# FFN weights loaded and first channels mixed sooner, a new place for the last two weights, and the last pair's gate columns ahead of the former pair's experts

## What is computed

```python
# 1 a long convolution per token channel h (64 of them) over the 1024 features, masked by a length
y = irfft(rfft(u_m, n) * rfft(kernel(h), n))[..., :L] + u_m * D[:, None];  y = y * mask
# 2 grouped-query attention, 32 query heads, 8 key/value heads of 32, causal, sequences of 64
q, k, v = y @ Wq.T, y @ Wk.T, y @ Wv.T;  q, k = rope(q), rope(k)
x = x + softmax(q @ k.T / sqrt(32) + causal) @ v @ Wo.T
# 3 channel mixing: each sequence's 64 tokens mixed by one of 16 matrices of 64 x 64
xf = einsum('bct,bcd->bdt', x, weights[condition])
# 4 a linear layer with a mixture of 8 rank-8 experts, the 2 best by a softmax gate
w = top2(softmax(xf @ gate_W.T)) normalised
x = x + xf @ W_base.T + einsum('ter,eor->to', (xf @ A) * w * 2.0, B)
```

## Time and profile before

| What | Value |
|---|---|
| Median of three runs (lowest to highest) | 924.44 us (922.88 to 925.8) |
| The profiled execution: its own time | 924.91 us |
| Its span in the profile | 922.8 us |
| TensorE busy | 881.5 us, 96% |
| VectorE, GpSimd, ScalarE busy | 446.4, 395.5, 202.4 us |
| Output store of 512 KB, issue to landing | 2.6 us, median |
| Store to the x1 scratch of 512 KB, issue to landing | 3.1 us, median |
| Instruction queues (q8 and q14) | 107 packets, 1.6 MB, 0.3% of the DMA time |

### The profile page before, as it was taken

The page is one execution under the profiler, slowest core; times in us unless marked ns, Lnnn a source line. Parts: engine busy times, 40 slices in busy tenths (PEclk is TensorE's granted clock), DMA queues, the critical chain, the costliest instruction groups (busy, mean ns, idle before and its releaser), DMA issues.

```text
span 922.8 us, 24871 instructions
## 1 busy us (share of the span) xinstructions
PE 881.5 (96%) x11040; PEld 766.8 (83%) x11040; DVE 446.4 (48%) x935; ACT 202.4 (22%) x363; POOL 395.5 (43%) x294
## 2 busy tenths in 40 slices
PE   0899999999999999999999999999999999999997
PEld 0789899988888888888777777777779999999997
DVE  7455663111222222259887776788514444334444
ACT  4334552200000000023123222233322111011010
POOL 1234555301555656569978877867511000000000
PEclk9999999999999999999999989999999999999999
DMA  2678878412223323256544544643343221212201
GB/s 65 150 190 205 203 177 191 119 46 69 69 77 97 78 69 75 51 172 178 152 138 138 154 140 137 180 133 113 136 132 107 70 92 47 92 70 70 93 24 69
DMA packets 81931, 105.35 MB, mean 114 GB/s; under 512 B 41505, under 2 KB 54433, under 8 KB 81825
## 3 DMA queue, kind: packets, MB, share of 16 engines
q1 hardware_dynamic: 81312, 103.24, 39.3%
q0 software_dynamic: 512, 0.53, 0.2%
HBM read 74.08 MB, written 29.65 MB: 112 GB/s over the span
## 4 chain that ended last, share of the span: by engine, by line
PE 91%; DMA 3%; DVE 2%; issue 1%; SPq 1%; POOL 1%; ACT 0%; DVEq 0%; POOLq 0%
PE ps L806 24%; PE ps L1262 20%; PE ps L1069 19%; PE ps L525 9%; PE ps L770 5%; PE ps L536 4%; PE ps L1004 3%; PE ps L1024 3%; PE ps L1230 2%; PE ps L1282 1%; DMA kpad<-ksb 1%; DMA wb_raw<-in_dram 1%; PE ps L1283 1%; DMA xc<-in_dram 1%; DMA toep<-kpad 0%
## 5 line engine op out<-in xcount | busy, mean ns | idle before, releaser
L1262 PE MATMUL ps<-wb,xf 128*128 128x420 f32 (+1 forms) x1152 | 195.4, 329 | 2.5 <-issue 1.6
L1262 PEld LDWEIGHTS ps<-wb,xf 128*128 128x128 f32 x1152 | 189.3, 188 | 5.9 <-issue 3.2
L806 PE MATMUL ps<-y_hi,w_hi 128*128 128x512 f32 x320 | 125.1, 391 | 0.0
L806 PE MATMUL ps<-y_hi,w_lo 128*128 128x512 f32 x320 | 124.5, 389 | 0.0
L806 PE MATMUL ps<-y_lo,w_hi 128*128 128x512 f32 x320 | 124.5, 389 | 0.0
L525 PE MATMUL ps<-xc,toep 64*128 64x192 f32 (+4 forms) x1088 | 101.5, 339 | 12.2 <-DMA toep<-kpad 8.2
L525 PEld LDWEIGHTS ps<-xc,toep 64*128 64x128 f32 x1088 | 93.4, 193 | 16.4 <-issue 13.0
L1069 PE MATMUL ps<-y_hi 128*128 128x512 f32 x256 | 104.1, 407 | 0.3 <-POOL y_lo L941 0.3
L1069 PE MATMUL ps<-y_hi,y_lo 128*128 128x512 f32 x256 | 101.2, 395 | 0.0
L1069 PE MATMUL ps<-y_lo,y_hi 128*128 128x512 f32 x256 | 101.2, 395 | 0.0
L913 POOL TENSOR_TENSOR rot<-rot,cst 128x512 f32<-128x512 f32 x40 | 52.7, 1318 | 72.8 <-DVE rot L884 72.8
(11 more groups left out here) (145 smaller groups left out, 1287.2 us busy)
## 6 DMA issues: line engine op xcount, KB each, us to landing
toep<-kpad SPq DMA_DIRECT2D x64, 272.0 KB, 4.9
xc<-in_dram SPq DMA_DIRECT2D x32, 256.0 KB, 5.1
q_rows<-rf SPq DMA_DIRECT2D x32, 256.0 KB, 2.6
q<-q_rows SPq DMA_DIRECT2D x16, 512.0 KB
xr<-in_dram SPq DMA_DIRECT2D x16, 512.0 KB, 4.6
x_scratch<-xr SPq DMA_DIRECT2D x16, 512.0 KB, 3.1
x<-x_scratch SPq DMA_DIRECT2D x16, 512.0 KB, 3.7
out_dram<-x SPq DMA_DIRECT2D x15, 512.0 KB, 2.6
```

Source lines behind the costliest of these rows:

```text
L806: mm = pe.matmul(kq_bank(n), w[a][:, j, :], yt[b][:, j, g * 512:(g + 1) * 512], start=(j == 0 and a + b == 0), stop=(j == NJ - 1 and a == 1))
L1262: mm = pe.matmul(joint_bank(i, piece)[:, 0:hi - lo], xf[i % 2][:, a, t, :], wb[t][:, c, lo:hi], start=(t == 0 and a + c == 0), stop=(piece ...
```

## The change

On SyncE, the loads of tiles 4 and 5 go ahead of the store of pair 14. Tiles 6 and 7 get new places (the first at the start of the area of the split output weights, the second 12288 values further in), and of their two halves the one that is free sooner takes the raw form (`w4_place`). Their loads no longer wait for all projections: the first waits for `project(15, 0)`, the second in addition for the store of pair 14, whose buffer it overlaps; both stand ahead of the store of pair 15. On TensorE, `mix_channels(0)` stands ahead of the whole of `project(15, 1)`, no longer behind its first 8 matmuls. For the last pair, the 12 matmuls of the gate's piece stand ahead of `experts(14)`, the other 24 behind it. On VectorE, the last addition of pair 14 goes behind the gate of pair 15.

```diff
         s4 = ExitStack()
+        WB_EARLY = 6
+        WB_6, WB_7 = 0, 6 * TOK
+        wb_late = [take(s4, "wb_6", [P, 2, NBASE], F32R)]
         x1_late = [take(s4, f"x1_{n}", [P, L]) for n in (2, 3)]
         xf_late = take(s4, "xf_1", [P, 2, NJ, P], F32R)
-        WB_EARLY = 6
-        wb_late = [take(s4, f"wb_{t}", [P, 2, NBASE], F32R) for t in range(WB_EARLY, NJ)]
+        fill(s4, "before_wb_7", WB_7)
+        wb_late += [take(s4, "wb_7", [P, 2, NBASE], F32R)]
...
                 if i == NPAIR - 1:
                     load_x1(sp, 0)
                     load_x1(sp, 1)
+                    sp.wait_ge(pe_o, NUNIT)
+                    for t in range(WB_FREE, WB_EARLY):
+                        load_w4(sp, t)
                 if i >= 1:
                     store_x1(sp, i - 1)
...
-            sp.wait_ge(pe_o, NUNIT)
-            for t in range(WB_FREE, WB_EARLY):
-                load_w4(sp, t)
+            sp.wait_ge(pe_y, 2 * NPAIR - 1)
+            load_w4(sp, 6)
+            sp.wait_ge(st_x1[(NPAIR - 2) % 3], 16 * ((NPAIR - 2) // 3 + 1))
+            load_w4(sp, 7)
             store_x1(sp, NPAIR - 1)
...
                 if w < NUNIT:
                     values_and_scores(pe, w)
-                if w < NUNIT + 1:
-                    project(pe, i, n)
-            project(pe, NPAIR - 1, 1, end=NQT)
-            mix_channels(pe, 0)
-            project(pe, NPAIR - 1, 1, first=NQT)
+                if w == NUNIT + 1:
+                    mix_channels(pe, 0)
+                project(pe, i, n)
...
+        def w4_place(t, part):
+
+            return part if t < WB_EARLY else 1 - part
+
         def load_w4(sp, t):
-            sp.dma_start(wb_raw[t][:, 1, :], w_ffn[:, t, :]).then_inc(ld_w4[t], 16)
+            sp.dma_start(wb_raw[t][:, w4_place(t, 1), :], w_ffn[:, t, :]).then_inc(ld_w4[t], 16)
 
         def ffn_transfers(sp):
             sp.wait_ge(pe_y, 2 * NPAIR)
-            load_w4(sp, WB_EARLY)
             for half in range(2):
                 sp.dma_start(bexp_raw[half * NH:(half + 1) * NH, :], w_b).then_inc(ld_p4, 16)
-            for t in range(WB_EARLY + 1, NJ):
-                load_w4(sp, t)
...
+                if i == NPAIR - 1:
+                    joint(pe, i, 1, (0,))
                 if i >= 1:
                     pe.wait_ge(a_p4, 1)
                     pe.wait_ge(g_p4, 1)
                     experts(pe, i - 1)
                 if i < NPAIR:
-                    joint(pe, i, 1)
+                    joint(pe, i, 1, (0, 1, 2) if i < NPAIR - 1 else (1, 2))
...
             for i in range(NPAIR + 1):
                 if i >= 1:
                     gate(v, i - 1)
+                if i == NPAIR:
+                    add_experts(v, i - 2)
+                if i >= 1:
                     v.wait_ge(a_hthi, i)
                     v.tensor_tensor(ht[NH:, :], turned_h(i - 1)[NH:, :], ht[NH:, :].bitcast(F32), ALU.subtract).then_inc(v_htlo, 1)
                 if i + 1 < NPAIR:
                     xf_lo(v, i + 1)
-                if i >= 1:
-                    v.wait_ge(v_base, i)
-                    for piece, (lo, hi) in enumerate(JOINT):
-                        v.wait_ge(pe_out, 3 * (i - 1) + piece + 1)
-                        x = x1[(i - 1) % 4][:, max(lo - NPROJ, 0):hi - NPROJ]
-                        total = joint_bank(i - 1, piece)[:, 0:hi - lo] if piece else own_experts(i - 1)
-                        v.tensor_tensor(x, total, x, ALU.add).then_inc(v_out, 1)
+                if i >= 1 and i != NPAIR - 1:
+                    add_experts(v, i - 1)
```

More of the change, by code:

```diff
@@ L245, in build @@
         s5 = ExitStack()
-        fill(s5, "before_wb_late", 2 * L + 2 * NJ * P)
-        raw_late = [take(s5, f"wb_raw_{t}", [P, 2, NBASE]) for t in range(WB_EARLY, NJ)]
+        raw_late = [take(s5, "wb_raw_6", [P, 2, NBASE])]
+        fill(s5, "before_raw_7", WB_7)
+        raw_late += [take(s5, "wb_raw_7", [P, 2, NBASE])]
         fill(s5, "before_wb", Y_END + 2 * NJ * P)
@@ L1053, in o_lo, with project @@
             v.tensor_tensor(o_heads(1, u, 1), o_banks(1), o_heads(0, u, 1).bitcast(F32), ALU.subtract).then_inc(v_otlo, 1)
[L1055 to L1064, removed]
+        def project(pe, i, n):
+            if n == 0:
+                pe.wait_ge(a_othi, 2 * i + 2)
+                pe.wait_ge(v_otlo, 2 * i + 2)
+            if i == 0:
+                pe.wait_ge(v_rcos, 4 * NU - 1 + n)
+            else:
+                pe.wait_ge(a_pr, 2 * (i - 1) + n + 1)
+            for at in range(3 * NQT):
                 t, (a, c) = at // 3, PASSES[at % 3]
@@ L1070, in project @@
                                start=(at == 0), stop=(at == 3 * NQT - 1))
-            if end == 3 * NQT:
-                mm.then_inc(pe_y, 1)
+            mm.then_inc(pe_y, 1)
         def attention_matmuls(pe):
@@ L1240, in own_experts, with joint @@
             return joint_bank(i, 0)[:, hi:hi + hi - NPROJ]
-        def joint(pe, i, half):
+        def joint(pe, i, half, pieces=(0, 1, 2)):
             if half == 0:
@@ L1250, in joint @@
                     pe.wait_ge(a_pr, 2 * NPAIR)
[L1251 to L1256, removed]
+            for t in range(half * 4, half * 4 + 4):
                 pe.wait_ge(a_w4, t + 1)
@@ L1261, in joint @@
                         lo, hi = JOINT[piece]
-                        mm = pe.matmul(joint_bank(i, piece)[:, 0:hi - lo], xf[i % 2][:, a, t, :], wb[t][:, c, lo:hi],
+                        mm = pe.matmul(joint_bank(i, piece)[:, 0:hi - lo], xf[i % 2][:, a, t, :], wb[t][:, w4_place(t, c), lo:hi],
                                        start=(t == 0 and a + c == 0), stop=(piece == 0 and t == NJ - 1 and a == 1))
@@ L1317, in w4_hi @@
             act.wait_ge(ld_w4[t], 16)
[L1318 removed]
+            act.activation(wb[t][:, w4_place(t, 0), :], wb_raw[t][:, w4_place(t, 1), :], ACT.Copy).then_inc(a_w4, 1)
         def w4_lo(v, t):
             v.wait_ge(a_w4, t + 1)
[L1322 removed]
+            v.tensor_tensor(wb[t][:, w4_place(t, 1), :], wb_raw[t][:, w4_place(t, 1), :], wb[t][:, w4_place(t, 0), :].bitcast(F32),
                             ALU.subtract).then_inc(v_w4, 1)
@@ L1404, in ffn_gates, with add_experts @@
                     xf_lo(v, i + 1)
-                if i >= 1:
-                    v.wait_ge(v_base, i)
-                    for piece, (lo, hi) in enumerate(JOINT):
-                        v.wait_ge(pe_out, 3 * (i - 1) + piece + 1)
-                        x = x1[(i - 1) % 4][:, max(lo - NPROJ, 0):hi - NPROJ]
-                        total = joint_bank(i - 1, piece)[:, 0:hi - lo] if piece else own_experts(i - 1)
-                        v.tensor_tensor(x, total, x, ALU.add).then_inc(v_out, 1)
+                if i >= 1 and i != NPAIR - 1:
+                    add_experts(v, i - 1)
+        def add_experts(v, i):
+            v.wait_ge(v_base, i + 1)
+            for piece, (lo, hi) in enumerate(JOINT):
+                v.wait_ge(pe_out, 3 * i + piece + 1)
+                x = x1[i % 4][:, max(lo - NPROJ, 0):hi - NPROJ]
+                total = joint_bank(i, piece)[:, 0:hi - lo] if piece else own_experts(i)
+                v.tensor_tensor(x, total, x, ALU.add).then_inc(v_out, 1)
         block = ctx.enter_context(nc.Block())
```

## The result

The changed kernel took 919.32 us (median of 21 runs, 915.27 to 922.89), the kernel before in the same series 922.88 us (21 runs, 919.26 to 926.52). The ratio is 0.9949 with a 95% interval of 0.9935 to 0.9964: 4.7 us faster, between 3.3 and 6.0. The two medians differ by 3.56 and the means of the two sets of 21 by 4.30, both inside that interval. Where this text says that 4.7 was measured, it means the ratio. The profiled execution has a span of 918.5 us against 922.8.

A forecast was written before the change was run, and what follows sets the result against it. TensorE, busy 96% of the span, was taken as the bound, so only its pauses and the tail could be won. 1.75 + 1.00 + 0.83 = 3.58 us off a median of 924.44 gave 920.8 us, range 919.2 to 922.9.

The forecast's parts named there:

- Term A: TensorE's pause before the first FFN product, put down to VectorE's late split of mixed channels, closes: 1.75 us.
- Term B: TensorE's wait in the FFN for weight tile 7 goes as its load is issued sooner: 1.00 us.
- the experts' factor: Next late after tile 7, ahead of pair 1's mixed channels: ready at 697.8, wanted at 698.1, thinly covered.
- Term C: Wait before the experts of pair 14, filled with 12 gate products: 0.83 us gained.
- VectorE's deferred addition: Last pair: pair 14's addition behind the gate ends at 915.9, with 0.7 us of cover before the last low part.
- The sum: Whole kernel: 1.75 + 1.00 + 0.83 = 3.58 us gained, bounds 2.4 to 4.0.
- The first (a pause that is not VectorE's): Before the first FFN product TensorE simply had no instructions, the pause stays: gain 1.83, 922.6 us; chance 0.07.
- the second (thin covers): At the seam, covers of 0.07 and 0.3 us fail, 0.5 lost at each: gain 2.6, 921.8 us; chance 0.10.
- The third: In the last pair, VectorE's deferred addition holds up the last low part: 921.6 us; chance 0.05.
- The fourth: At the seam, DMA load starves TensorE of instructions; pause and lost clock cost 4.8: 925.6 us; chance 0.05.

## Why the prediction was right in mechanism and short in size

**Term A** was 1.75 and measured 1.77. The releaser that the profile didn't name was the one worked out: with the load and the mixing both moved the pause went, with either alone it stayed. The working had VectorE's split end 18.47 us behind the start of the last values and TensorE free at 18.65; the split ended at 18.53 and the product started at 18.66. The wait closed as worked out, with hardly more room than the 0.07 that the text gave it.

**Term B** was 1.00 and measured 1.08 as a stretch. Its size is right and its attribution is not. The text took A and B as two waits to be added. Without the new places A's 1.77 come back in front of tiles 6 and 7, 2.0 us longer than before. B is what makes A worth anything. What was said to be late next, the experts' factor, was, and was covered.

**Term C** was 0.83 and measured 1.00: the twelve products start 0.03 behind the transpose, not 0.2. That VectorE's deferred addition is covered was right. That the deferral carried nearly the whole term was the expectation of a later run, and that run showed 0.2 us.

**The sum** is the step that failed, in two places: 2.1 us were forecast from where the kernel before stood, and 4.7 measured.

The first place is the start. The three terms give 3.6, but the forecast of 920.8 was hung on a median of 924.44 from three runs, where 21 runs gave 922.88. That takes 1.6 from the forecast gain. That 919.32 lies in the range of 919.2 to 922.9, and that the two medians differ by just 3.56, is luck.

The second place is the step that takes the waits of one profiled execution for those of the kernel, and has no term for the clock that the kernel before loses behind them. The stretches of the two profiles already differ by 3.93, by 0.17 in C and 0.1 each in B and in the FFN's steady part. The other 0.8 is not in these two profiles. Over the five traces of the kernel before, the way from the last values to the end is 0.9 us longer on the mean than in the one that the sum was made from. Of that, 0.1 lies behind the last transpose, where the changed kernel has it too. The rest, 0.77, lies before T0. The waits vary there, the pause in front of the first product from 1.62 to 2.03 (2.31 in the kernel with the last pair alone) and the wait for tile 7 from nothing to 2.01, but on the mean they add only 0.1. The 0.7 left is the clock: 1.7 us of full clock gone in two traces of five. In the changed kernel there is no wait at that place, none of its traces shows a lower clock there, and three of them agree to 0.3.

The time series bear this out. Each run has a span and a mean granted clock, and the span times what is missing of the clock is the full clock lost, wherever in the run, behind the last product too. Over the 80 runs of the kernel before that have both on record it is 3.4 us on the mean, over 39 of the changed kernel 2.6: 0.8 apart, some 0.6 each way. Less this loss the spans are 917.9 and 914.0, 3.9 apart, some 0.5 each way, which is what the waits explain. That part of the loss falls elsewhere, and that one series of 35 runs of the kernel before loses 2.8 and two others 3.7, makes it likely and not proved that all of the 0.8 is the seam's. Ahead of the seam no difference shows: the last values start at 664.5 on the mean of ten traces without the new places and at 664.3 in six with them, though single traces scatter too much (661.2 to 667.0) for this to settle tenths.

**The rivals.** The first (a pause that is not VectorE's) and the second (thin covers) are out. The third is out. The fourth, a starved TensorE at the seam, did not come in any of eight profiles with the earlier loads. Its price left out the 0.14 of the clock missing from 544 to 548, 0.6 us more. Its premise, that DMA load makes such pauses, found no support: with the DMA engines at a share of 0.04 the pause near 548 stayed. (The two instruction queues hold 0.8% of the time of 16 DMA engines in the profile before, not the 0.3% of the table of the kernel before.) The Trainium skill ("Runtime: NRT & Kernel Launch", Instruction fetch mechanics) holds the streaming of code to be mostly hidden. The run with later queries neither shows code fetch as the pause's cause nor rules it out.

Of the clock the traces show that it can fall to 1.2 GHz behind a pause of 2.0 us, 1.2 to 1.3 us after TensorE has started again. The Trainium skill ("TensorE: Matmul & The Clock Gate", Part 1) says that the clock is throttled when TensorE has been idle and released by activity. In two of the five traces of the kernel before, the trace agrees. The pauses of 2.31 and 2.52 with full clock behind them show that the length of a single pause doesn't settle it here. What does is open.

## What to carry to other kernels

A wait between engines, read in one trace, is one draw: before a gain of a few microseconds is sized by it, its chain should be asked how much it can vary (the wait for tile 7 was nothing in one trace and 2.0 in another), and removing it is worth the mean and not the draw. Here the mean of the waits was close to the draw and the clock behind them was not: the granted clock of every run tells such a loss where a single profile misses it. A forecast of a difference should start from as many runs as it will be compared with. Two waits that hang on one chain are not two terms: ask of each load what it would wait for if TensorE came sooner. Filling a wait with products that are needed anyway cost nothing here, where they had no wait of their own: T14 to T15 fell by 1.00.

## What the hardware showed that was not expected

Equal instructions reach the seam at 663.06 to 666.25 us in five traces of the kernel before. Near 548 (544 to 549) a pause of 1.7 to 2.8 us with no releaser stands in the traces of all kernels here. Behind it the clock is at half for nothing, for 3.4 or for 6.8 us: for nothing in the kernel with later queries behind 1.93 us of pause, and 0.50 and 0.78 over eight microseconds in the first trace behind the same 1.93. In the five traces of the kernel before, the start of the last values scatters by 3.2 us, and its single runs lie between 917.91 and 927.49: that is what hides differences of one microsecond between series.
